# Second attention: the cosine projection and the eight-column product in two parts each, with a head's score and turns between

## The reference

```python
Q, K, V = x @ Wq + bq, x @ Wk + bk, x @ Wv + bv      # 8 heads of 32 columns
qq, kq  = Q @ Wc2q + bc2q, K @ Wc2q + bc2q           # 8 columns a head
fid     = (qq @ kq.T) / max(|qq| * |kq|, 1e-8)       # cosine
qw      = fid * (1 + 0.1 * sin(pi * fid))
aw      = 0.5 * qw + 0.5 * (Q @ K.T) / sqrt(32)
attn    = softmax(aw) @ V @ Wo + bo
x1      = layernorm(x + attn)
qm      = (x1 @ W1 + b1) @ Wm + bm                   # 8 columns
ff      = ((tanh(qm) * cos(qm * pi / 4)) @ Wqo + bqo) @ W2 + b2
out     = layernorm(x1 + ff)
```

## Time and profile before

| | us |
|---|---|
| median of three runs | 3685.66 |
| the profiled execution | 3684.24 |
| its span | 3682.5 |
| TensorE busy | 3126.0 (85%) |
| VectorE busy | 2780.8 (76%) |
| ScalarE busy | 2189.1 (59%) |
| GpSimd busy | 1110.1 (30%) |
| mean granted clock of TensorE | 0.93 |

### The profile page before, as it was taken

How to read it: one execution, slowest core, us unless ns; L and a number is a source line. 1 busy time by engine, 2 the same in 40 slices (tenths; PEclk the granted TensorE clock), 3 DMA queues, 4 the chain that set the end, 5 groups by cost and what they waited for, 6 DMA issues and landing times. The chain is left out here.

```text
span 3682.5 us, 70565 instructions
## 1 busy us (share of the span) xinstructions
PE 3126.0 (85%) x24024; PEld 2426.3 (66%) x24024; DVE 2780.8 (76%) x7209; ACT 2189.1 (59%) x5360; POOL 1110.1 (30%) x664
## 2 busy tenths in 40 slices
PE   6899899899895799998588888888888885799998
PEld 4666666666664788887356555566655554688888
DVE  4676676666765888896478888888888884788986
ACT  3666666666672343433477777887777774334333
POOL 1000000000002455554233333443333343455553
PEclk9999999999996899999699999999999987899999
DMA  5244244343333000000334444443434442111000
GB/s 89 43 68 60 43 68 60 50 68 53 57 43 101 19 18 18 18 12 29 52 47 64 64 68 65 72 67 58 70 64 68 66 63 80 36 35 35 24 29 24
DMA packets 134182, 190.46 MB, mean 52 GB/s; under 512 B 15126, under 2 KB 81558, under 8 KB 133142
## 3 DMA queue, kind: packets, MB, share of 16 engines
q1 hardware_dynamic: 133830, 185.95, 29.8%
HBM read 45.65 MB, written 28.84 MB: 20 GB/s over the span
## 5 line engine op out<-in xcount | busy, mean ns | idle before, releaser
L405 ACT ACTIVATE a_probs<-a_probs,a_negmax 128x176 f32<-128x176 f32 (+4 forms) x1024 | 502.0, 491 | 334.7 <-DVE a_negmax L328 334.3
L328 DVE CUSTOM_DVE_ANT_0 a_probs<-a_mask,a_score 128x176 f32<-128x176 f32 (+4 forms) x1024 | 404.1, 400 | 224.7 <-PE a_score L479 100.2
L490 PE MATMUL a_turned<-ident,a_probs 128*128 128x128 f32 (+1 forms) x2176 | 428.8, 289 | 78.5 <-DVE a_pT L337 71.3
L1693 DVE CUSTOM_DVE_ANT_0 b_u<-b_u,b_score 128x512 f32<-128x512 f32 x512 | 340.4, 681 | 133.3 <-PE b_score L1938 130.8
L1230 PE MATMUL f_y_bank<-f_wdT,f_hqT 128*128 128x256 f32 x1536 | 362.0, 386 | 87.3 <-DVE xs L1101 84.9
L1812 ACT ACTIVATE b_u<-b_u,b_negmax 128x512 f32<-128x512 f32 x512 | 367.1, 717 | 109.5 <-DVE b_negmax L1693 108.1
L1685 DVE SCALAR_TENSOR_TENSOR b_u<-b_u,b_score 128x1024 f32<-128x1024 f32 x256 | 310.0, 1215 | 93.6 <-ACT b_u L1805 91.3
L1230 PEld LDWEIGHTS f_y_bank<-f_wdT,f_hqT 128*128 128x128 f32 x1536 | 286.7, 191 | 138.5 <-DVE xs L1101 101.4
L1805 ACT ACTIVATE b_u<-b_score 128x1024 f32<-128x1024 f32 x256 | 262.3, 1025 | 162.3 <-PE b_score L1928 161.8
L1160 ACT ACTIVATE f_h_mag<-f_hu 128x704 f32<-128x704 f32 x128 | 101.4, 792 | 429.1 <-POOL f_hu L987 429.1
L1947 PE MATMUL b_turned<-ident,b_u 128*128 128x128 f32 x2048 | 319.6, 281 | 26.8 <-DVE b_pT L1699 21.9
(11 more groups left out here) (233 smaller groups left out, 7155.1 us busy)
## 6 DMA issues: line engine op xcount, KB each, us to landing
b_stack<-b_part SPq DMA_DIRECT2D x192, 256.0 KB, 8.3
a_stack_q<-a_part SPq DMA_DIRECT2D x192, 128.0 KB, 4.4
a_stack_k<-a_part SPq DMA_DIRECT2D x192, 128.0 KB, 5.8
xs<-in_x_dram SPq DMA_DIRECT2D x16, 512.0 KB, 8.3
x_before_b<-xs SPq DMA_DIRECT2D x16, 512.0 KB, 2.9
b_xin<-x_before_b SPq DMA_DIRECT2D x16, 512.0 KB, 12.2
b_xres<-x_before_b SPq DMA_DIRECT2D x16, 512.0 KB, 3.8
x_after_b<-b_xres SPq DMA_DIRECT2D x16, 512.0 KB, 5.8
```

The source lines that it names most:

```text
L328: dve.tensor_tensor_reduce(out=probs[:, n % 2, j, 0:keys(n)], in0=mask_of(n), in1=score[j][:, 0:keys(n)], scale=-1.0, scalar=3.0e38, op0=A ...
L405: act.activation(probs[:, n % 2, j, 0:keys(n)], probs[:, n % 2, j, 0:keys(n)], ACT.Exp, bias=negmax[:, n, j:j + 1], scale=-1.0, accum_out= ...
L490: m = nc.tensor.transpose(turned[j % 2][0:rows, u, :], chunk(n, probs[:, n % 2, j, :], u), ident[:])
L1693: dve.tensor_tensor_reduce(out=u[:, n, j, :], in0=u[:, n, j, :], in1=score[:, j, :], scale=-0.05, scalar=3.0e38, op0=ALU.add, op1=ALU.min, ...
```

## The change

`B0` is cut into its two products and `m0` into two tiles and two tiles. The first part is issued by a new function `start_side`, at the place named in `B_STARTS`; the second part is what is left of the job in `do_side`, at a later step. `B0` had stood at (0, 3); its first product stays there and the second goes to (1, 1). `m0` had stood at (6, 2); its first half stays there and the second goes to (6, 3). `N0` goes from (1, 3) to (2, 0). The moves on VectorE and ScalarE are put later in their tables: `B0` on VectorE from (1, 0) to (1, 2), its squares on ScalarE from (1, 1) to (1, 3), `N0` on VectorE from (2, 0) to (2, 1), `m0` on VectorE from (6, 3) to (7, 0), and `spread_norms` from (4, 2) to (4, 3).

```diff
 B_JOBS = [
-    (0, 3, "B0", "S", 1),
-    (1, 3, "N0", "S", 1),
+    (1, 1, "B0", "S", 1),
+    (2, 0, "N0", "S", 1),
...
-    (6, 2, "m0", "S", -1),
+    (6, 3, "m0", "S", -1),
...
+B_STARTS = {(0, 3): "B0", (6, 2): "m0"}
...
-            MOVES = {(1, 0): "B0", (2, 0): "N0", (3, 3): "z1", (5, 1): "G0", (6, 3): "m0", (8, 3): "Q0", (10, 1): "K0", (10, 3): "t0",
+            MOVES = {(1, 2): "B0", (2, 1): "N0", (3, 3): "z1", (5, 1): "G0", (7, 0): "m0", (8, 3): "Q0", (10, 1): "K0", (10, 3): "t0",
...
-                        if (n, j) == (4, 2) and has(s + 1):
+                        if (n, j) == (4, 3) and has(s + 1):
                             spread_norms(s + 1)
...
-            MOVES = {(1, 1): "B0", (2, 3): "z0", (5, 1): "G0", (5, 3): "R0", (8, 3): "Q0", (9, 3): "R1", (10, 0): "K0", (13, 0): "V0",
+            MOVES = {(1, 3): "B0", (2, 3): "z0", (5, 1): "G0", (5, 3): "R0", (8, 3): "Q0", (9, 3): "R1", (10, 0): "K0", (13, 0): "V0",
...
+            def start_side(s, job):
+                side = bank["S"]
+                wait(pe, s_free["S"], b_count(s, "S", job) - 1)
+                if job == "B0":
+                    freed(pe, s - 1, "xT0")
+                    freed(pe, s - 1, "xT1")
+                    mm(side, w["wqk"][:, 0, 0:P], xT[:, 0, :], start=True, stop=False)
+                else:
+                    freed(pe, s, "z1")
+                    for t in range(2):
+                        for k2 in range(KC):
+                            mm(side[:, NQ * t:NQ * (t + 1)], zT[:, k2, t * P:(t + 1) * P], w["wm"][:, k2, :],
+                               start=k2 == 0, stop=k2 == KC - 1)
...
-                    if job == "B0":
-                        freed(pe, s - 1, "xT0")
-                        freed(pe, s - 1, "xT1")
...
-                    for k2 in range(KC):
+                    for k2 in range(1 if job == "B0" else 0, KC):
...
-                    freed(pe, s, "z1")
-                    for t in range(TILES):
+                    for t in range(2, TILES):
...
+                        start = B_STARTS.get((n, j))
+                        if start and has(s + B_OFFSET[start]):
+                            start_side(s, start)
                         if (n, j) in jobs:
                             do_side(s, jobs[n, j])
```

## The result

The changed kernel takes 3737.27 us (median of 4 runs, 3731.16 to 3741.76) where the kernel before takes 3686.45 (median of four, three of them those of the table above): a ratio of 1.0133, with a 95% interval of 1.0118 to 1.0148. It is slower by 50.8 us, where 19.6 had been forecast, and above the range of 3682 to 3724. The profiled execution took 3731.16 us, its span was 3729.4.

A forecast was written before the change was run, and what follows sets the result against it. No engine is full; attention b's chain from squares through `N0`, scores and `weigh` to maximum (2,2) bounds. Late squares +13.5, `m0` -0.9 and clock falls +7 give +19.6 on 3684.24, forecast 3705 us, range 3682 to 3724.

The forecast's parts named there:

- What bounds, and the carrying of a delay: Attention b: engines wait for each other; a delay in the chain from squares to maximum (2,2) reaches the body's end.
- Part 1: `B0` in two parts: maximum (1,0) 1.7 us sooner, second product mostly at full clock, gain shrunk to 0.25 us.
- Part 2: Squares and `N0`: `N0` 1.57 us later, score (2,1) 0.9 us late; cost 0.9 us a body, bounds 0.5 and 1.6.
- Part 3: Clock behind `N0`: falls in 10 of 15 bodies instead of 5, 1.4 us each, +7 us; bounds 5 and 15.
- Part 4: `m0` in two parts: maximum (7,0) gains 0.06 us a body; bounds 0 and 0.9 us gained.
- Part 5: Norms' spreading behind maximum (4,3): copy starts 0.6 us later, ends as before; 0, bounds 0.6 gained, 0.4 lost.
- A: Rival, faster: squares on ScalarE come early and `N0` waits for nothing; -22 us, 3664 us; chance 0.09.
- B: Rival, no change: the 0.9 us is swallowed by a wait further down; about 3686 us; chance 0.13.
- C: Rival, much slower: turns between `B0`'s halves delay the clock 3.4 us, second-half records 0.85 us apart; 3723 us; chance 0.10.

The follow-up runs named there:

- spread_back: The changed kernel with the spreading of the norms back at (4,2): 3718.22 us, 1.0100 of the kernel before.
- wait_filled: The changed kernel with two more 128x512 products, overwritten by `N0`, in TensorE's wait before `N0`: 3696.0 us, 1.0027 of the kernel before.
- early_squares: The changed kernel, cuts kept, with VectorE's `B0` and ScalarE's squares both at (1,1): 3664.22 us, 0.9942 of the kernel before.
- m0_alone: The kernel before with only `m0` in two parts and its VectorE move at (7,0): 3684.93 us, 0.9994 of the kernel before.
- moves_alone: The kernel before, nothing cut, with only the later places of `B0`, `N0` and the squares: 3720.91 us, 1.0095 of the kernel before.
- early_spread_back: The changed kernel with VectorE's `B0` and the squares at (1,1) and the norms' spreading back at (4,2): 3665.15 us, 0.9953 of before.
- before_kept: The kernel before with three useless 128x512 products a body in TensorE's waits at the body's end: 3681.89 us, 0.9987 of the kernel before.

## Why the prediction was wrong

The direction and the chain were right. What failed is the size of three terms, of which the number of falls weighs most: 17 us, then the wait (7) and the spreading (9.5).

1. **What bounds, and the carrying of a delay**: right. In the table above every delay stays to the last but one sine, the end of its rows.
2. **Part 1**: right in its order, wrong in one time. Maximum (1,0) came 1.7 us sooner, and score (1,2)'s record began 0.2 us behind where it was. Maximum (1,2) was forecast 5.8 us behind `B0`, and came at 6.3; with it `B0`'s bias, maximum (1,3) and the squares were 0.45 us later than forecast. The step behind it is that the second product "runs mostly at the full clock". I had read from one body that the low clock ends 4.2 us behind `B0`'s start. In eleven of the fifteen bodies of the changed kernel it ended at 5.0 to 5.4, and the second product began in it: its record is 1.33 us long where it is 1.02 at the full clock. Where the low clock ends at 4.3, the forecast holds. In such a body of spread_back, at 2816.69, the squares start 9.17 us behind `B0`, and 9.13 had been forecast (TensorE's rows, then ScalarE's):

```profile
2821.10 1.02 PE L1887 MATMUL b_spare<-b_xT,b_wqk 128*128 128x512 f32 x2
2821.56 0.80 PE L1949 MATMUL b_score<-b_stack 96*128 96x512 f32 x1
...
2825.86 0.61 ACT L1751 ACTIVATE b_rn<-b_base 128x512 f32<-128x512 f32 x1
```

3. **Part 2**: the right mechanism, mis-sized: 1.38 us a body instead of 0.9, so 20.7 us instead of 13.5. The difference is the 0.45 us by which the squares were later than forecast. The bound of 1.6 held it. (The 20.7 take the typical body for all fifteen; in two, with squares at 8.3, score (2,1) was not later at all.)
4. **Part 3**, the step that failed: "five more falls x 1.4 = +7". There were 8 more falls behind `N0` (13 instead of 5), and also 10 more at 20 to 32 us and 6 more at 55 to 70. I had counted only the kind that I was looking at, although and the 83.3 us between the `B0`s at 2465.8 and 2549.1 (a body with falls at 10, 27 and 64 us) could have told me that one fall may come with others. Of the 54.3 us, 20.7 are the wait and 15 x 0.63 = 9.5 the spreading; the other 24, by subtraction and not measured by themselves, are left for those 24 falls, 1.0 us each. At the prices of the table (1.5, 1.5 and 0.5) they would be 30, and the wait somewhat less, since not every body has it in full. wait_filled shows it from the other side: without the first falls the second are gone as well. But it is no strict chain: in early_squares the second and third come in five bodies without a first, and in wait_filled twelve third falls come with neither. My upper bound, 15 falls in all, was a bound on one kind, and so the range was too narrow.
5. **Part 4**: right, nothing (m0_alone; score (7,0) is 5.06 us late where score (6,0) is 5.08).
6. **Part 5**: forecast 0, measured 0.63 us a body, with falls behind it: spread_back is 19 us faster than the changed kernel. The copy's 1.60 us had been a meeting with GpSimd's addition, and I took it that they would still meet. In most bodies they don't when VectorE is delayed by more than GpSimd. (I had also read the copy as ending with the addition at 2410.36; by its row it ends at 2410.65.)

Of the rivals, A's condition was right: early_squares starts the squares 1.3 us before those of the kernel before and is faster, at A's price of 3664 us; maximum (2,1) comes 1.6 us sooner there, where A had 1.5. In the kernel as changed it was not met. B is out. C, that turns between the halves of `B0` keep the clock low for 3.4 us more, is not what happened, though half of its sign was seen: the two records of the second half start 0.66 to 0.85 us apart in eleven of fifteen bodies. But the low clock ended 5.4 us behind `B0`'s start at the latest, not at 7.6, and it lasts until 5.1 to 5.4 in four bodies of the kernel before too, where no turns stand there. moves_alone, also without them, loses most of the same time, and early_squares and early_spread_back, with them, lose none. The rule of the Trainium skill that was weighed for C (TensorE: Matmul & The Clock Gate, Part 4: PE-mode transpose) thus found no bearing here. For the fall behind `N0` the Trainium skill (the same page, section "Why this matters for your kernels") asks only that long idle gaps between bursts of products be avoided, and its limit lies above the gaps seen here. The trace is stricter: a gap of 2.0 us with `N0`'s small products behind it was followed by a fall in 13 of 15 bodies, one of 1.3 us in 5, and in before_kept gaps of 0.99 and 0.60 us one after the other in most.

What stays open is why the falls recur at the same three places, and why the low clock at a body's start reaches 1 us further in most bodies of the changed kernel. Ten bodies of the changed kernel in a row are of one length to 0.6 us and their falls at the same places to 0.5 us, while those of the kernel before wander by two to five; that a body's length decides it was not tested.

## What to carry to other kernels

When a small job is put off, put off only what needs it: follow its result to the next engine's queue, and look for the step where that engine idles anyway; here the same cuts gave 50 us lost or over 20 won by the place of one move on VectorE and one on ScalarE. Count TensorE's waits for what they do to its clock, at all places of the loop and not at the one that is changed: a wait of 2 us cost about as much by the falls that followed it as by itself, and useless products in it took 41 us off. A copy that is slow where it meets another engine's work is not a fixed cost: each delay between the two changes who meets whom.

## What the runs showed of the hardware that was not expected

Filling waits pays even where the work is thrown away: 1.7 us of useless products a body took some 40 us off the changed kernel, and three such products around the end of a body took early_spread_back from 3665.15 to 3649.2, with runs of before at 3685.03 and 3686.54.
